# Conv attention on one core: the softmax rows turned by VectorE in 32 x 32 blocks and written to DRAM in pieces of 33 floats, in place of a TensorE transpose and a ScalarE copy

## The reference

```python
x_n = (x - mean) / sqrt(var + 1e-5)                 # group norm, 32 groups of 12 channels
w = qkv_w @ x_n                                     # 384 x 1024; 12 heads of 32 channels
w_normed = w / max(sqrt(sum_n w*w), 1e-12)          # per channel, over the pixels
s = sum_d w_normed**2                               # 12 heads x 1024 pixels
Pi = softmax(s * temp, over the 12 heads)
Pi_n = Pi / (sum_n Pi + 1e-8)
dots = sum_n Pi_n * w*w                             # per channel
u = -(w * Pi) / (1 + dots)
y = x + out_w @ u + out_b
```

## Time and profile before

| what | value |
|---|---|
| median of 3 runs | 917.19 us (916.14 to 918.69) |
| the profiled execution's own time | 916.16 us |
| its span, first to last instruction | 914.3 us |
| TensorE matmuls busy | 878.0 us |
| VectorE busy | 720.4 us (79%) |
| ScalarE busy | 541.5 us (59%) |
| GpSimd busy | 225.5 us (25%) |
| mean granted TensorE clock | 0.991 of full speed |
| data moved by DMA | 154.39 MB, 169 GB/s over the span |

### The profile page before, as it was taken

How to read it: one execution, slowest core, us unless ns; L and a number is a source line. 1 busy time by engine, 2 the same in 40 slices (tenths; PEclk the granted TensorE clock), 3 DMA queues, 4 the chain that set the end, 5 groups by cost and what they waited for, 6 DMA issues and landing times.

```text
span 914.3 us, 14405 instructions
## 1 busy us (share of the span) xinstructions
PE 878.0 (96%) x4404; PEld 691.1 (76%) x4404; DVE 720.4 (79%) x1366; ACT 541.5 (59%) x740; POOL 225.5 (25%) x101
## 2 busy tenths in 40 slices
PE   4699999999999999999999999999999999999976
PEld 3568777777877777877777787777787777778754
DVE  7478877888887787887788888878788778888654
ACT  3465656765566675565676555667556567655621
POOL 1122333212333321233321233332123332113300
PEclk9899999999999999999999999999999999999997
DMA  7125544445544345554445554434555444454331
GB/s 270 58 72 209 189 162 153 154 185 207 209 151 180 132 170 204 209 189 161 154 148 187 207 209 147 186 133 170 200 209 185 164 156 148 185 207 142 141 140 70
DMA packets 36836, 154.39 MB, mean 169 GB/s; under 512 B 4306, under 2 KB 7762, under 8 KB 32850
## 3 DMA queue, kind: packets, MB, share of 16 engines
q1 hardware_dynamic: 36672, 154.17, 46.7%
q10 hardware_dynamic: 146, 0.00, 0.0%
HBM read 102.24 MB, written 51.92 MB: 169 GB/s over the span
## 4 chain that ended last, share of the span: by engine, by line
PE 93%; DVE 3%; DMA 1%; issue 1%; ACT 1%; DVEq 0%; SPq 0%; ACTq 0%
PE acc L466 86%; PE scores L546 5%; PE scores L554 1%; DVE stats L626 1%; DMA PIB<-pi 1%; DVE WS L729 1%; PE small L454 0%; DMA X<-in_x 0%; PE small L460 0%; DVE XL L676 0%; DVE UL L765 0%; PE acc L443 0%; DVE X L773 0%; ACT XH L393 0%; DVE WV L755 0%
## 5 line engine op out<-in xcount | busy, mean ns | idle before, releaser
L317 POOL TENSOR_TENSOR XL<-XN,XH 128x1024 fp32r<-128x1024 f32 x93 | 222.5, 2408 | 623.3 <-ACT XH L393 623.3
L365 ACT ACTIVATE WS<-acc 128x1024 f32<-128x1024 f32 x96 | 98.7, 1028 | 275.0 <-PE acc L466 274.7
L466 PE MATMUL acc<-UH,W2H 128*128 128x512 f32 x576 | 181.4, 398 | 7.9 <-ACT UH L355 7.9
L773 DVE SCALAR_TENSOR_TENSOR X<-acc,bias,X 128x1024 f32<-128x1024 f32 x96 | 118.3, 1260 | 85.8 <-PE acc L466 85.8
L466 PE MATMUL acc<-XH,W1H 128*128 128x512 f32 x576 | 183.9, 401 | 2.0 <-ACT XH L393 2.0
L466 PE MATMUL acc<-XH,W1L 128*128 128x512 f32 x576 | 180.6, 395 | 0.0
L466 PE MATMUL acc<-UH,W2L 128*128 128x512 f32 x576 | 180.2, 396 | 0.0
L466 PE MATMUL acc<-UL,W2H 128*128 128x512 f32 x576 | 150.3, 396 | 0.0
L466 PE MATMUL acc<-XL,W1H 128*128 128x512 f32 x576 | 147.0, 390 | 0.5 <-POOL XL L317 0.5
L466 PEld LDWEIGHTS acc<-UL,W2H 128*128 128x128 f32 x576 | 105.7, 188 | 33.8 <-issue 12.8
L466 PEld LDWEIGHTS acc<-UH,W2H 128*128 128x128 f32 x576 | 106.5, 190 | 29.5 <-ACT UH L355 8.5
(11 more groups left out here) (74 smaller groups left out, 469.6 us busy)
## 6 DMA issues: line engine op xcount, KB each, us to landing
PIB<-pi SPq DMA_DIRECT2D x96, 516.0 KB, 6.3
out_y<-X SPq DMA_DIRECT2D x96, 512.0 KB, 7.4
X<-in_x SPq DMA_DIRECT2D x31, 1536.0 KB, 6.3
pi<-PIT SPq DMA_DIRECT2D x32, 48.4 KB, 1.6
X<-in_x SPq DMA_DIRECT2D x3, 512.0 KB, 4.8
WV<-in_L_conv_qkv_w SPq DMA_DIRECT2D x1, 576.0 KB, 6.7
WS<-in_L_conv_out_w SPq DMA_DIRECT2D x1, 576.0 KB, 7.7
temp_row<-in_L_conv_temp ACTq DMA_DIRECT2D x1, 0.0 KB
```

The source lines that it names most:

```text
L317: pool.tensor_tensor(XL[:, t, :], XN[:, t, :], XH[:, t, :].bitcast(F32), ALU.subtract).then_inc(xl_done, 1)
L365: act.activation(square_tile(i, t), acc[:, t, :], ACT.Square, accum_out=sumsq[:, t:t + 1]).then_inc(squared, 1)
L466: last = pe.matmul(out[:, h * BANK:(h + 1) * BANK], w[:, k, m * P:(m + 1) * P], r[:, k, h * BANK:(h + 1) * BANK], start=(n == 0 and k == 0 ...
L773: dve.scalar_tensor_tensor(x_tile(j, t), acc[:, t, :], bias[:, t:t + 1], x_tile(j, t), ALU.add, ALU.add).then_inc(y_done, 1)
```

## The change

The softmax rows are turned by VectorE. PI is now written by VectorE into PSUM columns 128 to 223 (of the bank `scores`, whose columns 0 to 95 hold the exponentials), in the same order (head, block). VectorE's transpose then turns each 32 x 32 block of the 128 x 96 array by itself, so PIT[128, 3, 33] holds in partition 32 q + r, r = (head within the tile, block b), the 32 pixels of quarter q of block b; a reduction puts their sum in the 33rd column. Both join VectorE's chain in `softmax_divide`, which has 8 steps instead of 6. The transpose on TensorE and ScalarE's copy are dropped. The sync engine waits for the chain's end, issues three writes, one per tile, of 128 pieces of 33 floats (132 bytes) each, and spreads each tile when its write has landed. PIB becomes [128, 3, 32, 33]; dot and weigh read rows of 32 elements, and pi_tot sums 32 columns per tile instead of 8. VectorE waits before it overwrites PIT until the three writes of the image before have landed. `head_sums` waits for the whole softmax chain of the image before.

```diff
--- before.py
+++ after.py
@@ -44,7 +44,7 @@
 (GN_MEASURED, GN_AGGREGATED, GN_MEANS, GN_OFFSET, GN_SPREAD, GN_VARIANCES, GN_LOGGED, GN_SEEDED, GN_SCALED, GN_RESIDUE,
  GN_ROOTED, GN_STEPS) = range(1, 13)
 HEADSUM_STEPS = 3
-SM_SHIFTED, SM_STEPS = 3, 6
+SM_SHIFTED, SM_STEPS = 3, 8
 ATTENDED = 3 + 4
 U_STEPS = ATTENDED + 3
 
@@ -145,21 +145,19 @@
         SE = sb("SE", [P, BLOCKS, HEADS])
         ssum = sb("ssum", [P, BLOCKS])
         srec = sb("srec", [P, BLOCKS])
-        PI = sb("PI", [P, HEADS, BLOCKS])
-
-        PIT = sb("PIT", [HEADS * BLOCKS, P + 1])
-        PIB = sb("PIB", [P, T, BLOCKS, P + 1])
+        PIT = sb("PIT", [P, T, QUAD + 1])
+        PIB = sb("PIB", [P, T, BLOCKS * QUADS, QUAD + 1])
         pick = sb("pick", [P, T, HEADS])
         pi_tot = sb("pi_tot", [P, T])
         dots = sb("dots", [P, 4, T])
 
-        pi_dram = nc.dram_tensor("pi", [HEADS, BLOCKS * (P + 1)], F32).ap()
+        pi_dram = nc.dram_tensor("pi", [HEADS, BLOCKS * QUADS * (QUAD + 1)], F32).ap()
 
         acc = pb("acc", [P, T, N])
         scores = pb("scores", [P, BANK])
         ST = scores[:, N // QUADS:2 * N // QUADS].rearrange("p (b h) -> p b h", h=QUAD)
         EX = scores[:, 0:BLOCKS * HEADS].rearrange("p (b h) -> p b h", h=HEADS)
-        turned_pi = scores[0:HEADS * BLOCKS, N // QUADS:N // QUADS + P]
+        PI = scores[:, P:P + HEADS * BLOCKS].rearrange("p (h b) -> p h b", h=HEADS)
         small = pb("small", [P, BANK])
         temp_ps = scores[:, C:C + HEADS]
 
@@ -190,9 +188,7 @@
         scores_done = sem("scores_done")
         sm_step = sem("sm_step")
         exp_done = sem("exp_done")
-        pi_turned = sem("pi_turned")
-        pi_kept = sem("pi_kept")
-        pi_written = sem("pi_written")
+        pi_written = [sem(f"pi_written_{t}") for t in range(T)]
         pi_spread = [sem(f"pi_spread_{t}") for t in range(T)]
         u_step = sem("u_step")
         uh_done = sem("uh_done")
@@ -278,11 +274,14 @@
                 if has(j):
 
 
-                    sp.wait_ge(pi_kept, j.counts(1, 1))
-                    sp.dma_start(pi_dram.rearrange("h (b n) -> (h b) n", n=P + 1), PIT[:]).then_inc(pi_written, 16)
-                    sp.wait_ge(pi_written, j.counts(16, 16))
+                    sp.wait_ge(sm_step, j.counts(SM_STEPS, SM_STEPS))
                     for t in range(T):
-                        heads = pi_dram[t * HPT:(t + 1) * HPT].unsqueeze(0).to_broadcast([D, HPT, BLOCKS * (P + 1)])
+                        rows = pi_dram[t * HPT:(t + 1) * HPT].rearrange("h (b q n) -> q (h b) n", b=BLOCKS, q=QUADS)
+                        sp.dma_start(rows, PIT[:, t, :]).then_inc(pi_written[t], 16)
+                    for t in range(T):
+                        sp.wait_ge(pi_written[t], j.counts(16, 16))
+                        heads = pi_dram[t * HPT:(t + 1) * HPT].unsqueeze(0)\
+                            .to_broadcast([D, HPT, BLOCKS * QUADS * (QUAD + 1)])
                         sp.dma_start(PIB[:, t].rearrange("p b n -> p (b n)"), heads).then_inc(pi_spread[t], 16)
 
             def step(i):
@@ -397,13 +396,6 @@
                     if has(i):
                         act.wait_ge(sm_step, i.counts(SM_STEPS, SM_SHIFTED))
                         act.activation(EX, SE[:], ACT.Exp).then_inc(exp_done, 1)
-
-                def keep_pi():
-                    if has(i):
-                        act.wait_ge(pi_turned, i.counts(1, 1))
-                        if i.follows(1):
-                            act.wait_ge(pi_written, i.counts(16))
-                        act.activation(PIT[:, 0:P], turned_pi, ACT.Copy, accum_out=PIT[:, P:P + 1]).then_inc(pi_kept, 1)
 
                 square_w(0)
                 keep_w(0)
@@ -420,7 +412,6 @@
                 x_hi(0)
                 exponentials()
                 normalise(1)
-                keep_pi()
                 x_hi(1)
                 normalise(2)
                 x_hi(2)
@@ -538,8 +529,7 @@
                 pe.wait_ge(headsum_step, i.counts(HEADSUM_STEPS, HEADSUM_STEPS))
                 pe.wait_ge(squared, i.counts(T, T))
                 if i.follows(1):
-                    pe.wait_ge(sm_step, i.counts(SM_STEPS, 1 - SM_STEPS))
-                    pe.wait_ge(pi_kept, i.counts(1))
+                    pe.wait_ge(sm_step, i.counts(SM_STEPS))
                 for t in range(T):
                     for q in range(QUADS):
                         block_q = square_tile(i, t).rearrange("p (b q r) -> p q b r", q=QUADS, r=QUAD)[:, q]
@@ -547,12 +537,6 @@
                                          block_q, start=(t == 0), stop=(t == T - 1))
                 last.then_inc(scores_done, 1)
 
-            def turn_pi(i):
-
-                if has(i):
-                    pe.wait_ge(sm_step, i.counts(SM_STEPS, SM_STEPS))
-                    pe.transpose(turned_pi, PI[:].rearrange("p h b -> p (h b)"), identity[:]).then_inc(pi_turned, 1)
-
             def step(i):
                 if not has(i) and has(i - 1):
                     last_product(i - 1)
@@ -564,8 +548,7 @@
                 group_variances(i + 1)
                 second_product(i - 1, 0, {(2, 0): lambda: head_sums(i)})
 
-                turn_at = (1, 1) if has(i + 1) else (0, 0)
-                second_product(i - 1, 1, {turn_at: lambda: turn_pi(i)})
+                second_product(i - 1, 1, {})
                 second_product(i - 1, 2, {})
 
 
@@ -711,14 +694,16 @@
                 dve.wait_ge(exp_done, j.counts(1, 1))
                 link(dve.tensor_reduce(ssum[:], EX, AX_X, ALU.add))
                 link(dve.reciprocal(srec[:], ssum[:]))
+                link(dve.tensor_tensor(PI.rearrange("p h b -> p b h"), EX,
+                                       srec[:].unsqueeze(2).to_broadcast([P, BLOCKS, HEADS]), ALU.mult))
                 if j.follows(1):
-                    dve.wait_ge(pi_turned, j.counts(1))
-                link(dve.tensor_tensor(PI[:].rearrange("p h b -> p b h"), EX,
-                                       srec[:].unsqueeze(2).to_broadcast([P, BLOCKS, HEADS]), ALU.mult),
-                     follows=False)
+                    for t in range(T):
+                        dve.wait_ge(pi_written[t], j.counts(16))
+                link(dve.transpose(PIT[:, :, 0:QUAD], scores[:, P:P + HEADS * BLOCKS]))
+                link(dve.tensor_reduce(PIT[:, :, QUAD], PIT[:, :, 0:QUAD], AX_X, ALU.add), follows=False)
 
             def in_blocks(tile):
-                return tile.rearrange("p (b n) -> p b n", n=P)
+                return tile.rearrange("p (b n) -> p b n", n=QUAD)
 
             def dot(j, t):
 
@@ -726,7 +711,7 @@
                     dve.wait_ge(pi_spread[t], j.counts(16, 16))
                     dve.wait_ge(squared, j.counts(T, t + 1))
                     dve.wait_ge(scores_done, j.counts(1, 1))
-                    dve.tensor_tensor_reduce(in_blocks(square_tile(j, t)), PIB[:, t, :, 0:P],
+                    dve.tensor_tensor_reduce(in_blocks(square_tile(j, t)), PIB[:, t, :, 0:QUAD],
                                              in_blocks(square_tile(j, t)), 1.0, 0.0,
                                              ALU.mult, ALU.add, dots[:, 0, t:t + 1]).then_inc(u_step, 1)
 
@@ -738,7 +723,7 @@
                 if k > 0:
                     dve.wait_ge(u_step, j.counts(U_STEPS, T + k))
                 if k == 0:
-                    done = dve.tensor_reduce(total, PIB[:, :, :, P], AX_X, ALU.add)
+                    done = dve.tensor_reduce(total, PIB[:, :, :, QUAD], AX_X, ALU.add)
                 elif k == 1:
                     done = dve.scalar_tensor_tensor(both, total, SUM_FLOOR, dot_all, ALU.add, ALU.add)
                 elif k == 2:
@@ -753,7 +738,7 @@
                     dve.wait_ge(u_step, j.counts(U_STEPS, ATTENDED))
                     dve.wait_ge(w_kept, j.counts(T, t + 1))
                     dve.scalar_tensor_tensor(in_blocks(w_tile(j, t)), in_blocks(w_tile(j, t)), dots[:, 3, t:t + 1],
-                                             PIB[:, t, :, 0:P], ALU.mult, ALU.mult).then_inc(u_step, 1)
+                                             PIB[:, t, :, 0:QUAD], ALU.mult, ALU.mult).then_inc(u_step, 1)
 
             def u_lo(j, t):
```

## The result

The changed kernel takes **905.22 us** (median of 4 runs, 903.14 to 905.88) against 916.71 for the kernel before in the same comparison: a ratio of 0.9867, 95% interval 0.9845 to 0.9889. Forecast were 906.2 us and a range of 904.0 to 911.5. Its profiled execution took 905.02 us with a span of 903.2, where the one before had 914.3.

A forecast was written before the change was run, and what follows sets the result against it. TensorE was taken to bound the middle, with chains of single operations and DMAs deciding the ends. -9.9 (middle) - 1.1 (end) + 0 (start) = -11.0 us, from 917.19 to 906.2 us; range 904 to 911.5.

The forecast's parts named there:

- TensorE bounds the middle: Steady periods, images 2 to 29: TensorE is 96% busy and sets the 27.01 us period, which becomes 26.67.
- 30 x 0.33 = 9.9 us: Middle of the run: each of 30 TensorE transposes on the chain costs 0.33 us, so removing them gains 9.9 us.
- Rival (a): TensorE's middle: 0.16 of the 0.33 us may not be the transpose and may move on; 911.0 us, chance 0.10.
- VectorE's 0.60 us under its idle time: VectorE's new transpose (0.28) and reduction (0.26) with gaps add 0.60 us per image, covered by 2.25 us idle.
- Short rows at nothing: Dot and weigh on VectorE, six operations per image: reading rows of 32 instead of 128 costs 0.
- (c): Rival: short rows cost VectorE's dot and weigh 0.94 us per operation; +128 us, 1045 us, chance 0.03.
- The spreads 0.2 us earlier: Sync queue: the first spread goes at 448.8 against 449.02 us, as PIT is ready sooner.
- The landing of 1.6 us: Sync queue: each new short write of PIT lands in 1.6 us, the median of the present write.
- (b): Rival: short writes land late, dots wait for PIB, TensorE for headsum; 934 us at 4.0 landing; 0.06 slower, 0.04 same.
- 0.8 us of room: Loop from spreads through dots and headsum to the score matmuls: 0.8 us slack left per image in the worse period.
- The end, 1.1 us: Last image: TensorE's 0.86 us stall for PI and the 0.28 us transpose go, gaining 1.1 us.
- The start, 0: Image 0 to image 1's scores: -0.27 + 0.08 + 0.14 us, so 0 within 0.2.

The follow-up runs named there:

- late_turn: The kernel before, with its TensorE transpose moved one pair of matmuls later, ScalarE's copy and the single write kept: 911.85 us, ratio 0.9944.
- the dve runs: The changed kernel with extra VectorE reduction before the weigh operations, of 512 elements, 1024, or 1024 twice: 907.61, 918.89 and 955.26 us.
- warm_end: The changed kernel with seventy constant-data matmuls of 256 columns filling TensorE's idle time before the last image's product: 902.05 us, ratio 0.9855.

## Why the prediction was right

**TensorE bounds the middle**: right, with the period forecast at 26.67 and found at 26.66. **30 x 0.33 = 9.9 us**: 10.1. The size was right; what it was put down to was half wrong. The step took the whole 0.33 as the transpose's cost and called a part lateness; in fact the lateness is the larger part, 0.21 of 0.34. Rival (a) had this premise too, and failed in its conclusion: the gap did not move on to another matmul, since no other one waits there for fresh data. Its 911 us became true for late_turn instead, a kernel that keeps the transpose.

**VectorE's 0.60 us under its idle time**: right. 0.28 and 0.26 for the new operations; the wait for TensorE behind them fell from 2.25 to 0.9, 1.1 and 1.3 us in three periods of four (in the fourth it is 2.0 to 2.4 long, for the reason above). Two terms were mis-sized without effect: PI at 0.27, not 0.35, and pi_tot at 0.33, not 0.27. **Short rows at nothing**: right; (c) is out.

**The spreads 0.2 us earlier**: wrong. The landing of 1.6 us was taken from a write of 96 pieces. The three issues took 0.58 each, near the upper bound, and the first spread goes 2.18 behind the first write instead of 1.6. With the longer pi_tot it used much of VectorE's reserve, and a part of (b)'s sign came up, the dots that wait for PIB. It cost nothing because the **0.8 us of room** was nearly there: 0.76 and 0.66 by the dve runs, 0.75 in the mean of the trace. For the worse periods, for which it was worked out, it was too much: the worst had 0.38. It counted all of the 0.89 us between headsum and its matmuls, of which 0.20 are needed, and it had the spreads earlier. Nothing was late in the end, but by a smaller margin than forecast.

By the Trainium skill, "DMA: Bandwidth & Descriptors", Specifications, a transfer below 512 B becomes a read-modify-write. The prediction drew from it that the landing would be longer. It did get longer, but the packets in the traces show little of it in the pieces: the first write's 128 packets of 132 B take 14 ns each and run for 0.41 us in all, where the 96 of 516 B took 33 ns each and ran for 0.36. Of the 0.60 us more, 0.40 lie ahead of the first packet (1.23 us behind the issue's start for 0.83), 0.05 in the packets and 0.15 behind the last. No run has one write in short pieces, or three in long ones, so what makes the start later is open.

**The end, 1.1 us**: 1.14 up to the finish, then 0.13 and 0.34 given back, the second by a clock that the prediction did not look at. **The start, 0**: 0.3 gained in this pair of executions. In warm_end, whose start is that of the changed kernel, image 1's score matmuls begin at 62.06 instead of 63.89, so 0.3 is nothing. In the profiled execution the errors of the forecast, 0.2 us in the middle and 0.3 at the start one way and 0.4 at the end the other, cancel to 0.1 (11.1 for 11.0); that is luck, and the four runs of the changed kernel lie 2.7 us apart.

## What to carry to other kernels

An instruction at the head of an in-order queue that needs fresh data costs its wait as well as its work. In the matmul rows the wait does not stand as idle time, only as a longer distance between the pairs on both sides; the row of the weight load has it (0.43 us). A copy of the instruction on constants, and one that is moved a step later, tell the two apart in two runs. Room on an engine that is not the bound is a matter of the loop it closes, not of its idle share: here about 0.75 us per image out of 4.8 us idle (18% of 26.66). It is to be measured by how far the added work pushes its followers back, not by how long the added instruction runs. Where the bounding engine idles near the end of a program, filling it keeps its clock; here that gave 2.2 us in the trace, less than the medians can tell apart.

## What the hardware showed that was not expected

- VectorE's write of 96 elements with a stride of 8 floats takes 346 to 351 ns into SBUF and 266 ns into PSUM.
- A reduction of 96 elements at a pitch of 33 floats takes 329 ns, one of 96 elements from rows without such a pitch 255 to 258.
- Three DMAs of 128 pieces of 132 B take 0.58 us each to issue (first start to last end, by three), about as long as a spread of 528 KB (1.85 for three), and one of 96 pieces of 516 B takes 0.33.
- After 8 us of idle time TensorE's first 12 matmuls of 512 columns took 4.6 to 5.2 us in three executions, and 2.75 when fillers had kept it busy.
- 128 packets of 132 B go out in 0.41 us, 96 of 516 B in 0.36, but the first of them starts 1.23 us behind its issue's start instead of 0.83.
- On queue 14 the changed program fetches 8 KB of its instructions five times in each pass of the loop; the kernel before fetched nothing on it between 142.1 and 832.8 us.
